# A decoder layer on one core: decay product and row maximum of the first attention in one VectorE operation per head

## What is computed

```
x = layernorm(x + first_attention(x))
x = layernorm(x + second_attention(x, ctx))      # heads of 8 x 8, softmax over a gram matrix
x = layernorm(x + expert_layer(x))               # layernorm, router, top 2 of 8 experts

first_attention, for each batch, 16 heads of width 8:
    q = x @ W_q
    latent = (x @ W_k + x @ W_v) @ W_down_kv
    k, v = latent @ W_up_k, latent @ W_up_v
    scores = (q k^T / sqrt(128)) * decay          # 128 x 128 per head, decay = exp(-0.01 |t - t'|)
    out = softmax(scores) v @ W_o
```

## Time and profile before

| | us |
|---|---|
| median of 3 runs | 889.16 (888.18 to 890.44) |
| profiled execution, its own time | 885.5 |
| span of the profile, first to last instruction | 883.8 |
| TensorE busy | 646.6 (73%) |
| VectorE busy | 588.7 (67%) |
| GpSimd busy | 458.8 (52%) |
| ScalarE busy | 322.4 (36%) |

### The profile page before, as it was taken

How to read it: one execution, slowest core, us unless ns; L and a number is a source line. 1 busy time by engine, 2 the same in 40 slices (tenths; PEclk the granted TensorE clock), 3 DMA queues, 4 the chain that set the end, 5 groups by cost and what they waited for, 6 DMA issues and landing times. The chain is left out here.

```text
span 883.8 us, 14582 instructions
## 1 busy us (share of the span) xinstructions
PE 646.6 (73%) x3961; PEld 534.8 (61%) x3961; DVE 588.7 (67%) x1819; ACT 322.4 (36%) x756; POOL 458.8 (52%) x785
## 2 busy tenths in 40 slices
PE   1189988888889898989898530888888888885000
PEld 1057877777767676767677420777787878874000
DVE  2056886868687777778787433577777777774487
ACT  1034544444444443444444200444444444442000
POOL 9034547676666666666667671044343443434244
PEclk9999999999999999999999755899999999998555
DMA  8711111111111111111110000455555555551243
GB/s 196 146 43 40 43 43 31 52 35 48 37 45 38 45 37 46 46 37 55 28 49 16 16 24 20 152 167 165 151 171 159 171 163 157 176 167 52 79 120 92
DMA packets 86912, 74.18 MB, mean 84 GB/s; under 512 B 10896, under 2 KB 69840, under 8 KB 86832
## 3 DMA queue, kind: packets, MB, share of 16 engines
q1 hardware_dynamic: 76832, 60.14, 24.0%
q0 software_dynamic: 5392, 11.01, 4.0%
q10 hardware_dynamic: 4608, 2.10, 0.8%
HBM read 58.04 MB, written 15.17 MB: 83 GB/s over the span
## 5 line engine op out<-in xcount | busy, mean ns | idle before, releaser
L422 PE MATMUL ps_a<-vbd,pT 128*128 128x144 f32 x1024 | 149.8, 290 | 1.2 <-ACT pT L535 0.5
L422 PEld LDWEIGHTS ps_a<-vbd,pT 128*128 128x128 f32 x1024 | 134.8, 190 | 20.8 <-issue 15.5
L332 POOL TENSOR_TENSOR sc<-sc,rowmax 128x1024 f32<-128x1024 f32 x64 | 121.5, 1898 | 41.9 <-DVE rowmax L644 41.9
L431 PE MATMUL ps_s<-kbd,qT 128*128 128x512 f32 x256 | 132.6, 601 | 5.4 <-DMA kbd<-key_image 5.4
L638 DVE TENSOR_TENSOR sc<-ps_s,decay 128x512 f32<-128x512 f32 x128 | 87.4, 683 | 57.1 <-PE ps_s L431 56.4
L962 ACT ACTIVATE x2c<-ps_m,prt 128x256 f32<-128x256 f32 x117 | 55.5, 474 | 139.0 <-PE ps_m L927 139.0
L913 POOL DMA_INDIRECT expert_out<-yt,dest x78 | 82.8, 1062 | 34.3 <-issue 30.2
L938 PEld LDWEIGHTS ps_t<-wot,hid 128*128 128x128 f32 x624 | 92.6, 191 | 11.3 <-DVE hid L998 2.5
L535 ACT ACTIVATE pT<-ps_t 128x512 f32<-128x512 f32 x128 | 72.7, 596 | 70.0 <-PE ps_t L411 67.3
L925 PE MATMUL ps_m<-xg,w2t 128*128 128x256 f32 x234 | 74.0, 398 | 32.2 <-DVE hid L994 29.4
L938 PE MATMUL ps_t<-wot,hid 128*128 128x128 f32 x624 | 94.7, 275 | 1.9 <-DVE hid L998 1.9
(11 more groups left out here) (194 smaller groups left out, 1305.8 us busy)
## 6 DMA issues: line engine op xcount, KB each, us to landing
w2t<-in_L_ffn_W_dram SPq DMA_DIRECT2D x39, 256.0 KB, 2.7
w1t<-in_L_ffn_W_dram SPq DMA_DIRECT2D x39, 256.0 KB, 2.9
wot<-in_L_ffn_Wo_dram SPq DMA_DIRECT2D x39, 256.0 KB, 3.6
kbd<-key_image SPq DMA_DIRECT2D x128, 64.0 KB, 1.9
xst<-expert_in SPq DMA_DIRECT2D x39, 130.0 KB, 2.0
g<-expert_out SPq DMA_DIRECT2D x32, 128.0 KB, 2.1
xin<-in_x_dram SPq DMA_DIRECT2D x32, 64.0 KB, 2.0
xall<-in_x_dram SPq DMA_DIRECT2D x4, 512.0 KB, 6.7
```

The source lines that it names most:

```text
L332: pool.tensor_tensor(sc[:, slot], sc[:, slot], rowmax[:, slot, :].unsqueeze(2).to_broadcast([P, HALF, S]), ALU.subtract).then_inc(shifted, 1)
L422: mm = pe.matmul(acc, pT[:, quarter, j * S:(j + 1) * S], vbd[:, par, h, :], start=(h == 0), stop=(h == H - 1))
L431: pe.matmul(ps_s[:, quarter % 2, :, :], qT[:, par, :], kbd[:, par, 4 * quarter:4 * quarter + 4, :], start=True, stop=True).then_inc(scored, 1)
```

## The change

`v_decay` no longer multiplies four heads in one operation. For each of the four heads it issues one `tensor_tensor_reduce`: it multiplies 128x128 scores from PSUM with the decay matrix, writes the product to `sc`, and writes the maximum of each row to `rowmax`, starting the maximum from NEG. `v_max` and its semaphore are gone, with both calls. GpSimd's `shift` waits for the count of decayed quarters in place of the count of maxima. As `rowmax` is now written earlier, `v_decay` waits, ahead of a half, until the subtraction of two batches ago has read the old maxima.

```diff
--- before.py
+++ after.py
@@ -327,8 +327,7 @@
                     pool.tensor_tensor(rs[:, :], rs[:, :], mhalf[:, 0:1], ALU.pow).then_inc(done, 1)
 
                 def shift(b, half, slot):
-                    k = 2 * b + half + 1
-                    pool.wait_ge(maxed, k)
+                    pool.wait_ge(decayed, 4 * b + 2 * half + 2)
                     pool.tensor_tensor(sc[:, slot], sc[:, slot],
                                        rowmax[:, slot, :].unsqueeze(2).to_broadcast([P, HALF, S]),
                                        ALU.subtract).then_inc(shifted, 1)
@@ -634,14 +633,13 @@
                     slot = 2 * par + quarter // 2
                     dve.wait_ge(scored, 4 * b + quarter + 1)
                     before(dve, p_trans, 4 * (b - 2) + quarter + 1)
-                    j = 4 * (quarter % 2)
-                    dve.tensor_tensor(sc[:, slot, j:j + 4, :], ps_s[:, quarter % 2, :, :],
-                                      decay[:, :].unsqueeze(1).to_broadcast([P, 4, S]), ALU.mult).then_inc(decayed, 1)
-
-                def v_max(b, half, par):
-                    slot = 2 * par + half
-                    dve.wait_ge(decayed, 4 * b + 2 * half + 2)
-                    dve.tensor_reduce(rowmax[:, slot, :], sc[:, slot], AX.X, ALU.max).then_inc(maxed, 1)
+                    if quarter % 2 == 0:
+                        before(dve, shifted, 2 * (b - 2) + quarter // 2 + 1)
+                    for j in range(4):
+                        h = 4 * (quarter % 2) + j
+                        last = dve.tensor_tensor_reduce(sc[:, slot, h, :], ps_s[:, quarter % 2, j, :], decay[:, :], 1.0, NEG,
+                                                        ALU.mult, ALU.max, rowmax[:, slot, h:h + 1])
+                    last.then_inc(decayed, 1)
 
                 def step(b, par):
                     if on(b, 2):
@@ -718,8 +716,6 @@
                         dve.tensor_tensor(oh[:, par, :, :], iota_e[:, :].unsqueeze(1).to_broadcast([P, 2, E]),
                                           idx[:, par, 0:2].unsqueeze(2).to_broadcast([P, 2, E]),
                                           ALU.is_equal).then_inc(oh_ready, 1)
-                    if on(b, 0):
-                        v_max(b, 0, par)
                     if on(b, 3):
                         dve.wait_ge(gm_ready, b - 3 + 1)
                         dve.tensor_reduce(gmax[:, :], gm[:, :], AX.X, ALU.max, negate=True).then_inc(gmax_ready, 1)
@@ -757,8 +753,6 @@
                     if on(b, 2):
                         dve.wait_ge(stat1, b - 2 + 1)
                         dve.bn_aggr(mv1[:, :], st1[:, :]).then_inc(mean1, 1)
-                    if on(b, 0):
-                        v_max(b, 1, par)
                     if on(b, 2):
                         dve.wait_ge(rstd1, b - 2 + 1)
                         dve.tensor_scalar(x1[:, par, :], res1[:, :], mv1[:, 0:1], rs1[:, 0:1],
```

## The result

The changed kernel takes 901.72 us (898.96 to 903.91, 4 runs) against 888.95 us before on the same chip: ratio 1.014, 95% interval 1.0109 to 1.0171. It is slower, by 12.8 us. The forecast was slower by 28 us, 917 us, with a range of 885 to 946. The direction and the loop held; the size was more than twice too large, and two steps of the working failed.

What follows compares the result with a forecast made beforehand. No engine is full; a loop through quarter 1's score, VectorE to line 759, GpSimd to line 379 and TensorE bounds the step. 0.03 plus 1.53 less 0.48 is 1.08 us, times 26 is 28 us: 917 us, range 885 to 946.

Steps and rivals of the forecast that it cites:

- the loop: Score of quarter 1, VectorE to line 759, GpSimd to line 379, TensorE, next step: closes the 14.40 us step.
- The removed maximum: Half 0's maximum on VectorE, 1.13 us long: removing it gains only 0.48 us a step.
- line 737 takes line 728's place: On VectorE, GpSimd's subtraction (line 332) holds line 737 instead; quarter 2 starts 2.06 us after line 344's end, not 2.57.
- The fused quarters: VectorE's products: two instructions a head, 0.20 and 0.08 us, so 1.12 us a quarter, 0.51 more; quarters 1 to 3 cost 1.53.
- The lower end: Lower bound for VectorE's fused products: one instruction a head, 0.18 us, a quarter of 0.72 us.
- MATCH_VALUE_LOAD: VectorE's nearest short instruction without tensor result, 0.07 us start to start; basis for 0.08 us to put out the maximum.
- Quarter 0: First fused quarter on VectorE: idle time and overlap before quarter 1 cover 0.48 of its 0.51 us; 0.03 is left.
- Half 1's maximum: On VectorE behind line 759, in front of idle time: removing it gains nothing.
- The sum: Per step 0.03 plus 1.53 less 0.48, 1.08 us; times 26 is 28 us, median 917 us.
- Rival 2: VectorE's two instructions a head run in series, 0.46 us a head: 992 us; chance of more than 0.35 a head 0.09.
- rival 3: One instruction a head for VectorE's fused products, 0.18 to 0.20 us: 885 to 891 us; chance 0.12.
- rival 1: VectorE's line 737 gets in front of GpSimd's line 332: 877 us, or 867 with quarters of 0.80; chance 0.11.

Runs made afterwards that it cites:

- plain heads: Kernel before with each product done head by head, nothing fused, both row maxima kept: 904.06 us, ratio 1.0195.
- the maximum of a column: Kernel before with half 0's maximum taken over the first column of each head only: 880.91 us, ratio 0.9931.
- one copy: Changed kernel with one short GpSimd copy ahead of the subtraction of half 0: 896.17 us, ratio 1.0107.
- e2: Kernel before with half 0's maximum over each head's first column only, the removed maximum by itself: 880.91 us, ratio 0.9931.
- three copies: Changed kernel with three short GpSimd copies ahead of the subtraction of half 0: 867.35 us, ratio 0.9782.
- the kernel before with the wait: Kernel before, nothing fused, with GpSimd's subtraction of half 0 waiting for VectorE's last normalisation: 871.05 us, ratio 0.9813.
- two copies: Changed kernel with two short GpSimd copies ahead of the subtraction of half 0: 901.41 us, ratio 1.0163.

## Why the prediction was right in direction and wrong in size

*The loop* was right: score of quarter 1, VectorE to line 759, GpSimd to line 379, TensorE. From quarter 1 to line 759 it is 7.57 us before, 8.02 in the changed kernel, 8.15 with plain heads and 7.31 with the maximum of a column; the periods are 14.42, 14.86, 15.00 and 14.15, each 6.84 or 6.85 more. *No engine's busy time* told it: VectorE lost 24 us of work.

*The removed maximum* (predicted gain 0.48 us a step): measured 0.27 by itself. That it isn't 1.13 was right, and so was the reason, that the subtraction holds another operation in line 728's place. It was wrong about which one. The step that failed reads "line 737 takes line 728's place": the rows taken for it (line 764, started 0.16 us before a subtraction and free) were stretched to the 0.12 us that the prediction had between line 733 and the subtraction. It became 0.08, since the subtraction starts 0.12 us after line 344's end and not 0.16. The prediction had read its start, 316.40, as set by GpSimd's own queue; the maximum of half 0 ended at 316.32, and wherever that maximum is gone or short the subtraction starts 0.03 to 0.04 us earlier. At 0.08 line 733 is held, and line 737 then comes on top: quarter 2 starts 2.28 us after line 344's end and not 2.06. The run with one copy shows the predicted arrangement: there it is 2.15, with a subtraction 0.25 us behind line 344's end. Whether line 733 would have been held at 0.12 no run shows.

*The fused quarters* (predicted 1.12 us): measured 0.84 to 0.85. This is the term that was mis-sized, and the larger of the two errors. The main part at 0.20 was right (0.21), and so was the second instruction, but its 0.08 us isn't added: its row starts with the next head's. Taking 0.28 a head made 1.53 us of a term that measured 0.72 (3 times 0.24). The lower end, one instruction and 0.72 a quarter, was nearer than the value taken. MATCH_VALUE_LOAD was a poor stand-in: 0.07 us from its start to the next, for 0.01 of the accumulator's reading. Why they differ no run shows.

*Quarter 0* was right: the wait for TensorE covered it, with 0.16 or 0.17 us of it left in front of quarter 1.

*Half 1's maximum* was right: it lay in front of idle time. What was 2.77 us of it is now 0.93 and 2.78 in two places.

*The sum*: 0.03 plus 1.53 less 0.48, 1.08 us a step, should have been 0.72 less 0.28, 0.44 (e2's period gives 0.27, quarter 2's start 0.29). Times 26 this is 11.4 us of the 12.8 measured. The two errors pull opposite ways: the prediction charged 0.81 us a step too much for fusion (21 us) and gave 0.2 too much for the maximum (5 us), so the total is off by less than the fusion term alone. That is luck. Rival 2, the pair in series, and rival 3, no second instruction, both fell; rival 1, that line 737 gets in front of the subtraction, fell for this kernel. The kernel with three copies has its arrangement and even its 867 us, but that the numbers meet is chance: the figure was for quarters of 0.80 and nothing held, and there the scaled gram is held and quarters take 0.85.

*The Trainium skill.* Its statement that an operation with an accumulator output is two instructions ("VectorE: DVE Perf Modes", Two Vector instructions with no wait between them) agrees with the 512 READ rows. The Trainium skill's section The DRAIN you can't avoid of the same page, on which the prediction drew for rival 2, has the next operation wait for an empty pipe; it adds that an operation which is not held starts earlier. The rows go with the addition: a head's main row is 0.28 us long and the next head starts after 0.21. The Trainium skill's rule that the first to issue gets the shared ports for the whole instruction ("SBUF — State Buffer", Who interferes with whom) fits the kernel with one copy, where line 736 started 0.05 us behind the subtraction and was held, and the early step at 116.41 us of the kernel with three copies, where the subtraction gave way. It doesn't fit the starts of the 100 operations that began 0.08 to 0.10 us first and were held all the same; whether the start of a row is the moment of issue, no run shows.

## What to carry to other kernels

Before fusing a product with its row reduction, look whether it splits the product: here four operations of 128 elements in place of one of 512 cost 0.19 us a quarter, and that fell on the loop, while most of the saved reduction fell into a hold. Look for a row that takes several times what its shape takes elsewhere, and for what runs on GpSimd beside it, before removing work in front of it: a wait that moves GpSimd's long operation behind it gave 17 us, and with the next held operation moved too 25 us, where the fusion cost 13.

## What the runs showed that was not expected

- A VectorE operation of this kind (128x128, SBUF to SBUF, scalars per partition) that started 0.08 or 0.10 us before a long GpSimd operation was held to its end (2.06 us for 0.34) in 100 steps of 101; at 0.16 us and more it got through. The scaled gram (line 750 with three copies, 757 in the kernel before with the wait) started 1.4 and 1.0 us behind the subtraction's start and ended 0.08 us after its end, 0.57 and 0.95 us for 0.27. The fused products beside the same subtraction took their usual 0.28 us a head.
- Reading the accumulator on VectorE costs 0.01 us from head to head, though its row is 0.08 us long.
- In the profiled execution of the changed kernel TensorE's granted clock fell twice in the stage (0.58 and 0.68 as means over 3 and 5 us), and four steps there were 3.5 us longer together. In the kernel with one copy it fell once. The kernels with plain heads and with two copies idle about as long in front of the rank products (1.37 and 1.43 to 1.47 us) and have a mean clock of 1.00 in every step. What decides it stays open.
